# A kernel of attention and routed experts whose sample loops are written out on every engine

## What is computed

```python
x = L0_attn_x                                    # (32, 256, 128), float32
xn = layernorm(x)
qkv = einsum('bsm,qhdm->bqhsd', xn, W_qkv)       # (3, 16, 64, 128)
q, k = rope(qkv[:, 0]), rope(qkv[:, 1])          # the first 32 of 64 dimensions
attn = softmax(where(causal, -inf, q @ k.T) / 8)
a = concat_heads(attn @ v) @ W_o.T
probs = softmax(xn @ router_w + router_b)        # 9 choices
gates = one_hot_sum(top_k(probs, 2))
h = gelu(einsum('btd,edf->ebtf', xn, w1))        # 8 experts, 512 hidden
y = einsum('ebtf,efd->ebtd', h, w2)
out = x + a + einsum('bte,ebtd->btd', gates[..., :8], y) + gates[..., 8:] * xn
```

## Time and profile before

| | us |
|---|---|
| median of 3 runs | 1662.92 |
| lowest and highest of them | 1655.4, 1663.87 |
| the profiled execution's own time | 1659.1 |
| its span, first to last instruction | 1657.3 |
| the start, up to the first scores of sample 0 | 115.6 |
| samples 1 to 14 (first loop) | 580.70 |
| samples 17 to 30 (second loop) | 553.60 |

### The profile page before, as it was taken

How to read it: one execution, slowest core, us unless ns; L and a number is a source line. 1 busy time by engine, 2 the same in 40 slices (tenths; PEclk the granted TensorE clock), 3 DMA queues, 4 the chain that set the end, 5 groups by cost and what they waited for, 6 DMA issues and landing times.

```text
span 1657.3 us, 51489 instructions
## 1 busy us (share of the span) xinstructions
PE 1305.4 (79%) x15156; PEld 1004.5 (61%) x15157; DVE 1215.5 (73%) x4592; ACT 1132.0 (68%) x3606; POOL 812.2 (49%) x1324
## 2 busy tenths in 40 slices
PE   2517878787878787887799999887888787878787
PEld 1404656565656565665688898665656565656566
DVE  6698767676777777776577776886878687768785
ACT  7316757676666666777578887776767676767676
POOL 3234656555555655565000000665656565656565
PEclk9758989899898989999899999998999999989999
DMA  9512222222222222224122332232423232323330
GB/s 300 171 28 63 67 67 66 66 65 66 64 67 65 67 65 67 66 66 118 53 84 85 86 86 67 69 82 65 96 63 87 71 76 72 85 69 85 75 83 24
DMA packets 115934, 131.25 MB, mean 79 GB/s; under 512 B 11568, under 2 KB 75312, under 8 KB 115376
## 3 DMA queue, kind: packets, MB, share of 16 engines
q1 hardware_dynamic: 107056, 110.26, 26.4%
q0 software_dynamic: 8576, 17.33, 3.5%
HBM read 28.85 MB, written 31.59 MB: 36 GB/s over the span
## 4 chain that ended last, share of the span: by engine, by line
PE 35%; DVE 24%; issue 16%; DMA 12%; POOL 10%; ACT 2%; DVEq 1%; POOLq 0%; SPq 0%; ACTq 0%
PE bank L1120 7%; PE bank L1121 7%; PE bank L1122 6%; PE bank L1191 6%; DMA stage<-sorted_y_dram,rows_at 6%; DMA sorted_x_dram<-stage,rows_at 5%; DVE arena L974 5%; DVE arena L936 3%; PE bank L1201 3%; PE bank L1227 3%; DVE arena L947 2%; POOL arena L473 2%; POOL arena L493 2%; POOL arena L491 2%; DVE o_whole L1007 2%
## 5 line engine op out<-in xcount | busy, mean ns | idle before, releaser
L645 ACT ACTIVATE probs<-arena,neg_max 128x128 f32<-128x128 f32 (+1 forms) x1024 | 454.0, 446 | 200.8 <-DVE neg_max L974 198.3
L1191 PE MATMUL bank<-arena 64*128 64x128 f16 (+1 forms) x3072 | 184.2, 254 | 185.7 <-DVE neg_max L974 127.5
L974 DVE CUSTOM_DVE_ANT_0 arena<-bank,causal 128x128 f32<-128x128 f32 (+1 forms) x1024 | 316.7, 345 | 2.8 <-PE bank L1191 2.7
L503 POOL DMA_INDIRECT stage<-sorted_y_dram,rows_at x128 | 127.4, 995 | 260.9 <-DMA sorted_y_dram<-stage 238.5
L1201 PE MATMUL bank<-ident,probs 128*128 128x128 f32 x1536 | 249.6, 280 | 5.8 <-ACT probsT L628 5.0
L1191 PEld LDWEIGHTS bank<-arena 64*128 64x128 f16 x3072 | 103.3, 97 | 243.1 <-DVE neg_max L974 148.5
L985 DVE RECIPROCAL inv_total<-total 128x4 f32<-128x4 f32 x256 | 44.9, 175 | 241.6 <-PE bank L1191 238.9
L1201 PEld LDWEIGHTS bank<-ident,probs 128*128 128x128 f32 x1536 | 190.2, 146 | 40.7 <-issue 12.9
L472 POOL TENSOR_TENSOR arena<-arena 128x256 f32<-128x256 f32 x128 | 127.1, 993 | 165.3 <-DVE arena L936 165.2
L489 POOL TENSOR_TENSOR pause<-half 128x1 f32<-128x1 f32 x256 | 51.8, 202 | 307.0 <-DMA sorted_x_dram<-stage,rows_at 131.7
L628 ACT ACTIVATE probsT<-bank 128x384 f32<-128x384 f32 x384 | 185.2, 483 | 22.5 <-PE bank L1201 22.3
(11 more groups left out here) (155 smaller groups left out, 3447.0 us busy)
## 6 DMA issues: line engine op xcount, KB each, us to landing
arena<-arena SPq DMA_DIRECT2D x256, 256.0 KB, 4.7
arena<-sorted_x_dram SPq DMA_DIRECT2D x72, 128.0 KB, 2.1
sorted_y_dram<-stage SPq DMA_DIRECT2D x72, 128.0 KB, 1.8
sorted_x_dram<-arena SPq DMA_DIRECT2D x3, 2304.0 KB, 16.7
arena<-experts_dram SPq DMA_DIRECT2D x8, 512.0 KB, 5.1
out_dram<-acc SPq DMA_DIRECT2D x32, 128.0 KB
sorted_x_dram<-arena SPq DMA_DIRECT2D x1, 2368.0 KB, 16.3
sorted_x_dram<-stage,rows_at POOLq DMA_INDIRECT x128, 2.3
```

Source lines behind the costliest of these rows:

```text
L503: nc.gpsimd.indirect_dma_start(out=stage[:, k % BACKS, :], out_offset=None, in_=sorted_y[0:ROWS, :], in_offset=bass.IndirectOffsetOnAxis(a ...
L645: last = nc.scalar.activation(probs[:, s % 4, at:at + w], masked[:, s % 4, at:at + w], ACT.Exp, bias=neg_max[:, s % 4, t:t + 1], scale=-1. ...
L974: last = nc.vector.tensor_tensor_reduce(out=masked[:, s % 4, at:at + w], in0=SC[s % 2][:, at:at + w], in1=causal[:, at:at + w], scale=1.0, ...
L1191: last = mm(SC[h][:, at:at + w], q_stack[parity][rows, r, ql, u, qs], k_stack[parity][rows, r, kl, u, 0:w], start=(n == 0), stop=(n == 2))
```

## The change

The two functions that call `sample` are written out in Python, with the same order of samples and the same `parity` and `at` for each. `b` is then a number everywhere, so that waits compare with constants and addresses are fixed, and the loop's branch and counter are gone on all five engines. The expert loops stay as they are. The start, the expert tiles and samples 0, 15, 16 and 31 are not touched.

```diff
--- before.py
+++ after.py
@@ -266,21 +266,19 @@
 
             return (t_out[0], 4 * b + s // 4 + 1) if s % 4 == 0 else (t_out[1], 12 * b + s - s // 4)
 
-        def former_samples(eng, body):
+        def former_samples(body):
 
 
             body(0, 0, OPENING)
-            with eng.Fori(0, MID // 2 - 1) as i:
-                body(2 * i + 1, 1, FORMER)
-                body(2 * i + 2, 0, FORMER)
+            for b in range(1, MID - 1):
+                body(b, b % 2, FORMER)
             body(MID - 1, 1, TURN)
 
-        def latter_samples(eng, body):
+        def latter_samples(body):
 
             body(MID, 0, REOPEN)
-            with eng.Fori(MID // 2, B // 2 - 1) as i:
-                body(2 * i + 1, 1, LATTER)
-                body(2 * i + 2, 0, LATTER)
+            for b in range(MID + 1, B - 1):
+                body(b, b % 2, LATTER)
             body(B - 1, 1, FINAL)
 
         def beside(b, at, s):
@@ -391,7 +389,7 @@
                 tiles_at = slice(TPS * b, TPS * b + TPS) if isinstance(b, int) else bass.ds(TPS * b, TPS)
                 sp.dma_start(out_tiles[:, tiles_at, :], acc[:, tiles_at, :]).then_inc(stored, 16)
 
-            former_samples(sp, sample)
+            former_samples(sample)
 
 
             def load(i, k):
@@ -420,7 +418,7 @@
                 body(n, False)
             body(TILES // BODY - 1, True)
 
-            latter_samples(sp, sample)
+            latter_samples(sample)
             store_own(B - 1)
             sp.wait_ge(stored, 16 * 2 * (B - MID))
 
@@ -535,11 +533,11 @@
                     if (s - SPLIT_LAG) % 2 == 1:
                         o_split(8 * b + (s - SPLIT_LAG - 1) // 2, (s - SPLIT_LAG) // 2, b % 2)
 
-            former_samples(pool, sample)
+            former_samples(sample)
             rest_of(MID - 1)
             for done in ys_out:
                 pool.wait_ge(done, 16 * TILES // 2)
-            latter_samples(pool, sample)
+            latter_samples(sample)
             rest_of(B - 1)
 
 
@@ -673,7 +671,7 @@
                 o_copy(8 * b + 6, 6)
                 o_copy(8 * b + 7, 7)
 
-            former_samples(act, sample)
+            former_samples(sample)
             act.wait_ge(s_ready, 8 * MID)
             for e in range(EARLY, E):
                 split_high(e)
@@ -719,7 +717,7 @@
             body(TILES // BODY - 1, False, True)
             output(TILES - 1, BODY - 1, False)
 
-            latter_samples(act, sample)
+            latter_samples(sample)
             rest_of(B - 1)
 
 
@@ -1066,7 +1064,7 @@
                     n = len(units_of(at)) + t
                     y_add(b, t, unit_base(b, at) + n, PJ[n % PJ_BANKS], at == TURN)
 
-            former_samples(dve, sample)
+            former_samples(sample)
             rest_of(MID - 1, TURN)
             dve.wait_ge(y_done, TPS * MID)
             for e in range(EARLY, E):
@@ -1106,7 +1104,7 @@
                 body(n, False, False)
             body(TILES // BODY - 1, False, True)
 
-            latter_samples(dve, sample)
+            latter_samples(sample)
             rest_of(B - 1, FINAL)
 
 
@@ -1254,7 +1252,7 @@
                     n = len(units_of(at)) + t
                     unit("y", t, b, b % 2, PJ[n % PJ_BANKS], before(b, at, n))
 
-            former_samples(pe, sample)
+            former_samples(sample)
             rest_of(MID - 1, TURN)
 
             def tokens(i, k):
@@ -1323,7 +1321,7 @@
             e = two_bodies(TILES // BODY // 2 - 1, False, True)
             down(TILES - 1, e, BODY - 1, False)
 
-            latter_samples(pe, sample)
+            latter_samples(sample)
             rest_of(B - 1, FINAL)
```

## The result

The median went from 1663.39 us (1655.4 to 1669.14) to 1555.81 us (1554.54 to 1561.09): a ratio of 0.9362 with a 95% interval of 0.9317 to 0.9407. The forecast was 1569 in a range of 1540 to 1605. The medians lie 108 us apart, the spans of the two profiled executions 105 us (1657.3 - 1552.7), where the sum said 92. Some executions ran much slower at a lower granted clock, such as the profiled one of the loops with two turns (1718 us, clock 0.73), and the ratios leave them out.

What follows compares the result with a forecast made beforehand. No engine was saturated; TensorE's stops at the loops' jumps back were taken as the cost. Savings of 49 us (first half) and 43 (second) made span 1565; 1.8 around it and 2 for the median gave 1569, range 1540 to 1605.

Steps and rivals of the forecast that it cites:

- The stops are fetches of code: At each jump back TensorE stops twice, 2.46 and 2.80 us, read as fetching code for a long loop body.
- 7.4 us a jump: Gross cost of each of twelve jumps on TensorE: stops of 2.5 + 2.6 us, slower matmuls 2.3 us; 89 us in all.
- Registers 0.9 and 0.2 us a sample: Register work for waits and addresses in the loops, seen on VectorE: 0.9 us a sample first half, 0.2 second.
- First half 38.0 us a sample: Samples 1 to 14: TensorE asks 37.4 us, the sending chain 37.2; 38.0 each, 532 us, saving 49.
- rival 1: First half: GpSimd's sending chain replaces the stop, needing sample 10's 41.0 us; saves only 7 us there, total 1611; chance 0.13.
- Second half 36.5 us a sample: Samples 17 to 30: mean of samples 17 and 30, 36.65, less 0.2 for registers; 511 us, saving 43.
- The clock rival: TensorE's mid-sample clock dips: none left gives 1540 us, a double one each sample 1598; chance 0.12 for each end.
- The other engines' branches: Loop branches on engines besides TensorE: said to lie under TensorE's stop and go with it, costing nothing.
- Code fetch in straight code: Written-out TensorE stretches: fetch cost taken as 0; as a rival, a stop for each of 102 packets, 1834 us, chance 0.03.
- Packets down by two a jump to 120: Sign of being right: TensorE's instruction packets fall from 145 by about two per jump, to some 120.
- Change does nothing: Rival: TensorE's stop is something straight code has too, a table or queue; 1663 us, chance 0.03.
- Only jumps count: Rival: removing register work in the loops gains nothing, 15 us stay; 1584 us, within the range, sharing the forecast's 0.57 chance.

Runs made afterwards that it cites:

- the loops with two turns: Kernel before, each loop on all engines two turns of six samples, last two samples of each half written out: ratio 0.9533, 1588 us.
- The loops with four and two jumps: Kernel before with three turns of four samples a loop (1598.84 us, 0.9599) or two of six (0.9533), last two samples of each half written out.
- The late wait: Changed kernel with GpSimd's wait for the landing of the previous send moved to right before the send: 1549.93 us, ratio 0.9321.
- the first experiment: Kernel before with TensorE's stream alone written out, the other four engines keeping their loops: 1606.68 us, ratio 0.9678.

## Why the prediction was right, point by point

*The stops are fetches of code.* Shown. They end when the turn is short enough, with the loop, its registers and its branches in place, and the packets go with them. The queue of 145 packets is TensorE's, as it was read: it went to 110 when TensorE alone was written out. The Trainium skill's page Runtime: NRT & Kernel Launch (section Instruction fetch mechanics) says that straight code is refilled while it runs and that a taken branch out of the window waits for a fetch; the trace agrees in kind on both counts, with 28 written-out samples that show no stop, and 208 against 3479 ns. The window of two pages of 256 instructions that the Trainium skill gives in the same section is smaller than the turn of 1232 matmuls and loads that TensorE jumped back over without a stop; the measurement decides.

*7.4 us a jump.* Held in size. It is gross, and a little high. The pairs give (9.25 - 4.38) + (5.27 - 3.04) = 7.1 for the first half, less 0.4 of registers in pair 1, and (8.50 - 3.98) + (5.61 - 3.64) = 6.5 for the second. The forecast doesn't rest on it, as it priced samples without a jump. The loops with four and two jumps can't tell 6.5 from 7.4.

*Registers 0.9 and 0.2 us a sample.* 0.9 held, by medians: even samples of the first half lost 0.41 in pair 1, 0.21 in pair 2 and 0.19 in pair 5, 0.8 in all, odd ones 0.3 more in pair 4. In the second half it is 0.24 + 0.12 - 0.05 + 0.02 = 0.3, not 0.2. The reading that VectorE carries them held too.

*First half 38.0 us a sample.* Measured 37.7; 528.0 against 532. TensorE's 37.4 and a little for the sending chain were the right two terms. The late wait shows each: with it, 37.4 in the usual sample; without, some 0.5 more in the mean. From the first addition to the end of the next sample's first send the chain takes 35.2 to 39.3 us in the changed kernel, never the 41.0 of sample 10, so rival 1 as priced (1611) is out. What it named is real, and its sign, GpSimd's idle time near zero, came in 8 of 14 samples, but it is worth 6 to 7 us.

*Second half 36.5 us a sample.* Measured 35.95, 503.3 against 511, and this is where most of the extra gain is: the first half gave 52.7 us for 49, the second 50.3 for 43, the rest of the span 1.6 for nothing. The step that was off is the price taken as the mean of samples 17 and 30, one with a low-clock stretch and one without. That assumes half the samples to have one; 3 of 14 did, and (0.5 - 0.21) x 1.6 = 0.5 us a sample is about the miss. It is partly chance: the second profile of the same kernel has 6 of 14 and 36.2 us a sample. That two samples stood so well for fourteen is luck too. The clock rival had named this term, at 1540 if no stretch was left.

*The other engines' branches.* The sentence was right for this change and hid a number that it should have given. They do lie under TensorE's stop, and they went with it because all five engines were written out at once. The cover was never priced: once TensorE's stops alone are gone, VectorE's cost 1.5 and 2.4 us a jump in the pair behind it, and with the registers some 42 us in all, two fifths of the gain. A change that wrote out TensorE alone, forecast by the same reasoning, would have been missed by 30 us, as the first experiment was.

*Code fetch in straight code: 0.* Held; no gap of a microsecond at even spacing. *Packets down by two a jump to 120*: three a jump, to 110. The count of 209 instructions a packet took those 35 packets in, and also the expert loop's turns, which need no new ones. *Clock from 0.92 to 0.95*: 0.947. *Change does nothing*: excluded by the total. *Only jumps count*: excluded by pair 5, which keeps its register work in the looped samples and loses it in the written-out ones of the same trace.

## What to carry to other kernels

Before a hardware loop is written out, count what its longest engine issues in a turn and look at that engine's branch record: at 0.2 us that engine's jump is nearly free, at 3.5 us each jump pays 6 to 7 us here. Cutting the turn under the limit takes that stop away; it leaves the registers and the other engines' stops, and what it gives in time wasn't measured. The branch record doesn't show every stop: VectorE's is 63 ns. When several engines loop together, their stops cover each other, so undo them together and price each alone. A gain as large as this uncovers what the stops had hidden, here waits for sends and gathers: moving those by a step or two was worth another 1.8%.

## What the runs showed of the hardware

- TensorE jumps back in 208 ns with 616 matmuls and as many loads in a turn, and in about 3500 with 760; at 1520 (four samples) three of four jumps take 3499 to 3842 ns and one 5082. With 760 a jump costs it two stops, 2.0 to 3.0 us before the first scores and 2.4 to 3.1 us after two or three of them.
- VectorE stops for 2.3 to 3.2 us at its own jump, though its branch record shows 63 ns: here the stop is only visible as idle time before an instruction in the pair behind the jump, and three packets of code go with it.
- VectorE's reciprocal starts 0.27 us after the scores where its wait has a register and 0.17 where it has a constant. All register work together is 0.9 us a sample in one half and 0.3 in the other; that it counts only where TensorE waits for VectorE is a reading, not shown.
